# Expert tiles spread over four rounds each, results scattered by token: attention and a mixture of experts on one core

## What is computed

```
# attention, 16 heads of 8
scores = einsum('bhid,bhjd->bhij', q, k) / sqrt(D) * cos_mat
w = softmax(scores); w = (w + roll(w, 1)) / sqrt(2)
out = (w @ v) @ Wo
# experts: 8, the two best for each token, weights = softmax of their two logits
top_logits, idx = top_k(logits, 2); scores = softmax(top_logits)
h1 = x_rep @ w1[e].T; a, g = split(h1, 2)
he = (silu(a) * g) @ w2[e].T          # only where expert_ids == e
combined = (out * scores).sum over the two choices
```

## Time and profile before

| | |
|---|---|
| median of 3 runs | 619.6 us (619.36 to 619.75) |
| time of the profiled execution | 618.71 us |
| its span, first to last instruction | 616.7 us |
| PE busy | 558.7 us (91%) |
| ACT busy | 523.8 us (85%) |
| DVE busy | 200.1 us (32%) |
| POOL busy | 86.5 us (14%) |
| mean granted clock of PE | 0.98 |

### The profile page before, as it was taken

The page is one execution under the profiler, slowest core; times in us unless marked ns, Lnnn a source line. Parts: engine busy times, 40 slices in busy tenths (PEclk is TensorE's granted clock), DMA queues, the critical chain, the costliest instruction groups (busy, mean ns, idle before and its releaser), DMA issues.

```text
span 616.7 us, 19178 instructions
## 1 busy us (share of the span) xinstructions
PE 558.7 (91%) x8012; PEld 260.5 (42%) x8012; DVE 200.1 (32%) x493; ACT 523.8 (85%) x487; POOL 86.5 (14%) x95
## 2 busy tenths in 40 slices
PE   2968988898899999999999999999999988888885
PEld 1433322232355545555555555555455432233334
DVE  7954550200122434334243433424344100000413
ACT  2758879999698988989999898989988899999991
POOL 5200053445100000000000000000000044450000
PEclk9978997899899999999999999999999999999999
DMA  8650052212664333333423234342331011110002
GB/s 231 190 193 10 5 138 78 71 37 70 165 166 131 91 93 87 110 111 91 131 81 104 86 111 112 96 121 75 108 93 49 15 32 31 36 35 10 3 1 72
DMA packets 58666, 53.49 MB, mean 87 GB/s; under 512 B 28188, under 2 KB 48182, under 8 KB 58322
## 3 DMA queue, kind: packets, MB, share of 16 engines
q1 hardware_dynamic: 56082, 47.73, 27.5%
q0 software_dynamic: 2048, 4.20, 2.3%
q10 hardware_dynamic: 448, 0.30, 0.3%
HBM read 38.55 MB, written 13.63 MB: 85 GB/s over the span
## 4 chain that ended last, share of the span: by engine, by line
PE 67%; ACT 15%; issue 11%; DMA 2%; SPq 2%; DVE 2%; ACTq 0%; DVEq 0%
PE ps L1308 32%; PE ps L1282 20%; ACT big L681 14%; PE ps L1219 6%; PE ps L1229 4%; PE ps L1121 2%; PE ps L1315 1%; DMA qk_parts<-store 1%; DVE store L767 1%; DMA acc<-in_L_attn_x 1%; PE ps L1257 1%; ACT second L642 1%; SPq L431 1%; PE ps L1106 1%; DMA store<-in_L_ffn_w 0%
## 5 line engine op out<-in xcount | busy, mean ns | idle before, releaser
L681 ACT ACTIVATE big<-ps 128x1536 f32<-128x1536 f32 (+1 forms) x410 | 480.6, 1240 | 49.6 <-PE ps L1282 47.3
L1308 PE MATMUL ps<-big,vh 128*32 128x256 f32 (+1 forms) x3968 | 270.0, 397 | 0.0
L1282 PE MATMUL ps<-qa,ka 49*128 49x512 f16 x896 | 166.8, 391 | 28.1 <-ACT big L681 19.5
L1308 PEld LDWEIGHTS ps<-big,vh 128*32 128x32 f32 x3968 | 108.2, 110 | 120.3 <-issue 73.8
L1282 PEld LDWEIGHTS ps<-qa,ka 49*128 49x128 f16 x896 | 37.5, 94 | 141.1 <-ACT big L681 98.7
L1219 PE MATMUL ps<-xgT,store 128*32 128x128 f32 x1716 | 65.5, 273 | 2.4 <-DMA store<-in_L_ffn_w 2.4
L1219 PEld LDWEIGHTS ps<-xgT,store 128*32 128x32 f32 x1716 | 53.9, 110 | 17.5 <-issue 5.4
L565 POOL COPY vh<-vaug 128x144 f32 x16 | 6.6, 411 | 338.2 <-PE ps L1308 320.8
L935 DVE SCALAR_TENSOR_TENSOR cs<-cs,ps 128x384 f32<-128x384 f32 x39 | 21.6, 554 | 93.2 <-ACT cs L673 93.2
L971 DVE COPY osb<-ps 128x512 f32<-128x512 f32 x16 | 11.0, 688 | 113.9 <-PE ps L1308 113.8
L988 DVE TENSOR_REDUCE m<-ps 128x1 f32<-128x512 f32 x64 | 44.1, 689 | 5.4 <-PE ps L1325 5.4
(11 more groups left out here) (166 smaller groups left out, 212.0 us busy)
## 6 DMA issues: line engine op xcount, KB each, us to landing
store<-in_L_ffn_w SPq DMA_DIRECT2D x39, 352.0 KB, 3.0
store<-in_L_ffn_w SPq DMA_DIRECT2D x39, 192.0 KB, 3.4
qk_parts<-store SPq DMA_DIRECT2D x8, 512.0 KB
qa<-qk_parts SPq DMA_DIRECT2D x27, 128.0 KB
slots_x<-vh SPq DMA_DIRECT2D x5, 512.0 KB, 6.1
cs<-slots_x SPq DMA_DIRECT2D x80, 32.0 KB, 2.5
slots_y<-y SPq DMA_DIRECT2D x19, 128.0 KB, 3.0
ka<-qk_parts SPq DMA_DIRECT2D x31, 64.0 KB, 2.3
```

The costliest lines, as they stand in the source:

```text
L681: nc.scalar.activation(probs[:, prob_of(tiles[0]):prob_of(tiles[-1]) + 1, :], ps[:, bank_of(tiles[0]):bank_of(tiles[-1]) + 1, :], ACT.Exp, ...
L1282: ins = nc.tensor.matmul(ps[:, bank_of(n), :], k[at:at + KQ, P * o:P * o + P], q[at:at + KQ, CW * c:CW * c + CW], start=True, stop=True, t ...
L1308: ins = nc.tensor.matmul(ps[32 * c:32 * c + 32, O_BANKS[p % 2], cols], vh[:, p % 2, o + 8 * b, :], probs[:, prob_of(n), cols], start=k == ...
```

## The change

- `expert_step` gives a tile four rounds, the steps in the first three and none in the fourth. EXPERTS_AT goes from 41 to 37, so that tiles run in rounds 37 to 193.
- PAIR_EXP_AT goes from 3 to 0, TOP_EXP_AT from 12 to 7, RANK_AT from 8 to 7, SCATTER_AT from 16 to 11.
- Each row of `slots_x` has 132 elements in place of 128: the token's two weights, its first slot and its number (`place_tokens` in round 8, four small copies after `gates`). The zeros that fill `slots_x` go out in 8 DMAs in place of 5, and one more constant is loaded.
- SP loads those four elements of every row (`carried`, 39 pieces of 16 bytes on each of 128 partitions) behind the weights of the first three tiles. From them DVE works out in round 40 each row's weight and the DRAM row for its result (`rows_of_results`, ten instructions on 128x39).
- `result_out` multiplies by that weight. POOL scatters each tile's result to DRAM `results` by token and choice (`scatter_result`, 39 indirect DMAs); `store_results` and the 32 gathers are gone.
- At the end of SP's rounds four plain DMAs of 512 KB load the results, and DVE adds them in 8 instructions (`add_results`, in program order at quad 252, behind `normalise` of head 14).
- `load_exact_shifts` stands at round 156 of SP's program in place of its end.

```diff
-PAIR_EXP_AT = 3
-TOP_EXP_AT = 12
-RANK_AT = 8
+PAIR_EXP_AT = 0
+TOP_EXP_AT = 7
+RANK_AT = 7
+GATES_AT = 8
-EXPERTS_AT = 41
-SCATTER_AT = 16
-ROUNDS_A_PAIR = 6
+EXPERTS_AT = 37
+SCATTER_AT = 11
+ROUNDS_A_TILE = 4
...
-            pair_of, at = divmod(r - EXPERTS_AT, ROUNDS_A_PAIR)
-            m, step = 2 * pair_of + at // 3, at % 3
-            return (m, step) if 0 <= m <= TILES and at < 6 else (None, None)
+            m, step = divmod(r - EXPERTS_AT, ROUNDS_A_TILE)
+            return (m, step) if 0 <= m <= TILES and step < 3 else (None, None)
...
                     for first in range(STAGES - 1):
                         stage_weights(first)
+                    sp.dma_start(carried[:], slots_x[0:TILES * P, DM:WITH_PLACE].rearrange("(n p) k -> p n k", p=P)).then_inc(carried_ld, 16)
...
+            def load_results():
+                for i in range(4):
+                    sp.wait_ge(y_wr[i], -(-(TILES - i) // 4) * 16)
+                for q in range(4):
+                    sp.dma_start(gathered[:, 4 * q:4 * q + 4, :, :], results_v[:, 4 * q:4 * q + 4, :, :]).then_inc(results_ld, 16)
...
+            def scatter_result(m):
+                if m == 0:
+                    pool.wait_ge(rows_of_ready, 1)
+                pool.wait_ge(y_copied, m + 1)
+                nc.gpsimd.indirect_dma_start(results, bass.IndirectOffsetOnAxis(ap=row_of[:, m:m + 1], axis=0),
+                                             y[:, m % 4, :], None).then_inc(y_wr[m % 4], 16)
...
-                nc.vector.tensor_copy(y[:, m % 4, :], ps[:, SIDE_BANK, FP:FP + DM]).then_inc(y_copied, 1)
+                nc.vector.tensor_scalar(y[:, m % 4, :], ps[:, SIDE_BANK, FP:FP + DM], weight_of[:, m:m + 1], None,
+                                        ALU.mult).then_inc(y_copied, 1)
...
-                if r == EXPERTS_AT - 1:
-                    gates()
+                if r == GATES_AT:
+                    place_tokens()
+                if r == EXPERTS_AT + 3:
+                    rows_of_results()
```

More of the change, by code:

```diff
@@ L54 @@
 FP = NF * P
+WITH_PLACE = DM + 4
 ROWS = 2 * D
@@ L88 @@
 EARLY = HALF_HEADS - EXACT
-GATHER_AT = 200
+EXACT_AT = 156
+ADD_AT = 12
 ISQ8 = float(1.0 / np.sqrt(D))
@@ L433, in load_rows, with load_exact_shifts @@
                                  ).then_inc(xg_ld[half], 16)
[L435 to L440, removed]
+            def load_results():
[3 more added lines that the diff above has]
+                    sp.dma_start(gathered[:, 4 * q:4 * q + 4, :, :], results_v[:, 4 * q:4 * q + 4, :, :]).then_inc(results_ld, 16)
+            def load_exact_shifts():
+                sp.wait_ge(exact_shift_ready, 1)
+                for r in range(EXACT):
+                    for half in range(2):
+                        sp.dma_start(qe[64 * half:64 * half + 1, r, :].rearrange("o (t p) -> o t p", p=P),
+                                     exact_shift[NT * r:NT * r + NT, :]).then_inc(exact_shift_ld, 16)
             def stage_weights(m):
@@ L505, in _ @@
                     load_rows(m // 2 + 2)
[L506 to L514, removed]
+                if r == EXACT_AT:
+                    load_exact_shifts()
+            load_results()
             def attend_whole():
@@ L580, in _ @@
             pool.wait_ge(slot_ready, 1)
+            pool.wait_ge(placed, 4)
             def scatter_rows(j):
@@ L583, in scatter_rows @@
                 nc.gpsimd.indirect_dma_start(slots_x, bass.IndirectOffsetOnAxis(ap=slot[:, r, t:t + 1], axis=0),
-                                             xn[:, t, :], None).then_inc(scattered, 16)
+                                             xn_placed[:, t, :], None).then_inc(scattered, 16)
+            result_at = {RING * result_round(m) // NC + 1: m for m in range(TILES)}
             for w in range(SCATTER_AT, H * QUADS):
@@ L596, in _ @@
                     head_values(w // QUADS + 1)
[L597 to L605, removed]
+                if w in result_at:
+                    scatter_result(result_at[w])
         @block.scalar
@@ new lines, in rows_of_results @@
+            def rows_of_results():
+                dve.wait_ge(carried_ld, 16)
+                gate_1, gate_2, first_slot, token = (carried[:, :, k] for k in range(4))
+                here, spare = places[:, NT:NT + TILES], places[:, NT + TILES:NT + 2 * TILES]
+                then(nc.vector.tensor_tensor(choice[:, 0, :], first_slot, here, ALU.is_equal))
+                then(nc.vector.tensor_tensor(choice[:, 1, :], first_slot, here, ALU.not_equal))
+                then(nc.vector.tensor_tensor(choice[:, 2, :], choice[:, 0, :], gate_1, ALU.mult))
+                then(nc.vector.tensor_tensor(choice[:, 3, :], choice[:, 1, :], gate_2, ALU.mult))
+                then(nc.vector.tensor_tensor(weight_of[:], choice[:, 2, :], choice[:, 3, :], ALU.add))
+                then(nc.vector.scalar_tensor_tensor(choice[:, 2, :], token, -2.0, choice[:, 1, :], ALU.add, ALU.add))
+                then(nc.vector.scalar_tensor_tensor(choice[:, 3, :], token, 0.0, choice[:, 2, :], ALU.is_gt, ALU.mult))
+                then(nc.vector.scalar_tensor_tensor(choice[:, 4, :], token, 0.0, spare, ALU.is_equal, ALU.mult))
+                then(nc.vector.tensor_tensor(choice[:, 2, :], choice[:, 3, :], choice[:, 4, :], ALU.add))
+                nc.vector.tensor_copy(row_of[:], choice[:, 2, :]).then_inc(rows_of_ready, 1)
@@ L968, in copy_out, with add_results @@
+            def add_results():
+                dve.wait_ge(results_ld, 4 * 16)
+                for r in range(2):
+                    for q in range(4):
+                        if r == 1:
+                            dve.wait_ge(y_added, q + 1)
+                        here = acc[:, 4 * q:4 * q + 4, :]
+                        nc.vector.tensor_tensor(here, here, gathered[:, 4 * q:4 * q + 4, r, :], ALU.add).then_inc(y_added, 1)
             def copy_out(p):
@@ L1017, in _ @@
                         make_exact_shift(p)
-                    if p == H - 1 and k == JOB_QUAD:
-                        for j in range(2 * NT):
-                            add_result(j)
+                    if p == H - 1 and k == ADD_AT:
+                        add_results()
                 if step == 0:
```

71 lines of the change are left out of this document (38 added, 33 removed).

## The result

| | before | the change |
|---|---|---|
| median of 4 runs each | 619.67 us (619.36 to 620.84) | **610.71 us** (610.23 to 611.72) |
| ratio | | **0.9854**, 95% interval 0.9835 to 0.9873 |
| time of the profiled execution | 618.71 us | 611.17 us |
| its span | 616.69 us | 609.37 us |
| mean granted clock of PE | 0.980 | 0.973 |

Forecast were 609.2, between 604 and 614. The profiled executions are 7.5 us apart and the medians 9.0.

The account below looks back on a forecast made before the run. PE was taken as the bound for the 117 expert rounds and ACT behind them. Terms -12.1 + 2.0 + 0.3 + 0 - 0.6 = -10.4 took 618.71 to 608.3 us, median 609.2, range 604 to 614.

Parts of the forecast that it names:

- Four rounds a tile: Expert rounds: four rounds take 10.30 us in place of 10.61, -0.31 over 39 tiles, -12.1 us; bounds -29 and -3.5.
- heads: Expert rounds: three more head changes, 0.66 us each, fall in PE-bound rounds, +2.0 us, ends 0 and +2.0.
- the wait of 0.22: Expert rounds: PE waits 0.22 us for ACT to free a bank, in a round following one of about 2.4 or less.
- the fourth round gives nothing: Rival on expert rounds: each even round keeps a wait, a tile takes 10.6, heads' 2 us are paid: 620 us, chance 0.06.
- The way to the first tile: First widening, round 38: PE stands 2.7 us until the weights land, +0.3 us against before, ends -4 and +3.
- The carried rows: Load of 4992 pieces behind three tiles' weights: landed at 160 to 162, on the edge, 0 us, ends 0 and +4.
- The price by count: Load of the carried rows: priced by number of pieces, from 5120 pieces taking 7.41 us, at 7.2 us.
- The pair exponential: Early rounds: moving it from round 4's way to behind round 0 saves 0.6 us, ends -1.0 and 0.
- The ranks then come in time for round 7: Early rounds: with the pair exponential moved, the ranks are ready for round 7; no size given.
- Results: End of kernel: the results' load and eight additions finish by 594, before the last head's sum at 602.36, so 0 us.
- slower: PE's clock: Rival: a light round in every four idles PE, half-clock stretches cost 5 us a stage, 624 us with three; chance 0.05.
- The start stands no longer: Rival at the first widening: weights land before 149, the 2.7 us wait and half clock go, -4.5, 605 us; chance 0.12.

Follow-up runs that it names:

- experiment 1: The change with three rounds a tile in place of four, the carried rows' ten instructions one round earlier: 621.73 us, ratio 1.0024 to before.
- experiment 2: The change with EXPERTS_AT 38 in place of 37, so each tile's light round has two pieces of values: 628.74 us, ratio 1.0128 to before.
- Experiment 4: On one chip, the change unedited: 607.97 us; and the change with the first tiles' weights loaded ahead of the first rows: 602.99 us.
- experiment 7: The change with only PAIR_EXP_AT put back from 0 to 3: 611.92 us, ratio 0.9926 to before.
- experiment 6: The change with the front's numbers as before (pair exponential 3, top 12, rank 8, scatter 16, experts 41): 611.18 us, ratio 0.984 to before.
- experiment 5: The change with EXPERTS_AT 39 in place of 37: 605.11 us, ratio 0.9747 to before; with EXPERTS_AT 45: 617.13 us, ratio 0.9959.
- experiments 3: The change with SP staging the first three tiles' weights ahead of the rows: 605.55 us, ratio 0.9769 to before.

## Why the prediction held, and where it was off

Forecast were -10.4 us. The medians moved by 9.0 and the spans of the two profiles by 7.3; only the second can be followed through rows. The fourth round gave about what was forecast. What is missing lies in the clock (points 2 and 6) and in point 4.

1. **Four rounds a tile, -12.1, and heads, +2.0.** The period of 10.30 came out at 10.29, round by round. Round 38 to 204 took 8.86 us less; 1.6 more were lost at the start of the tiles (point 2), so tiles and heads gave 10.4, for 10.1 forecast. The period measured makes -12.5 over 39 tiles, which leaves +2.0 for the heads; no run separates the two. Taking the fourth round back (experiment 1) gives 9.1 and not 10.4, so 1.3 us of this are not shown to be its doing. The reasoning (the wait of 0.22 follows a round of 2.4 or less, and the pieces' parity decides where) also gave the sign of experiment 2 and nearly its size (628.7 for 632). The rival "the fourth round gives nothing, 620" is excluded by experiment 1.

2. **The way to the first tile, +0.3: mis-sized.** The stall itself was right (3.02 for 2.7). Both of its ends came some 2 us later than forecast (PE at 150.8, the weights at 153.8), most of it because round 38 began 1.6 us later than before. The step that failed is "the clock then falls or not as before". It fell for 6.8 us and not 3.4. The two rounds around the stall took 7.51 and 4.39, 6.65 over their steady 5.25; before, 7.23 and 3.31, 5.06 over theirs. So +1.6, of which 0.6 are the longer stall and 1.0 the clock. Experiment 4 shows that this varies by execution: where the half clock lasted 3.4 us, rounds 38 and 39 took 1.4 less.

3. **The carried rows, 0.** Landed before 161.3, as taken (160 to 162), and on the edge, as said: a wait of 0.28 us, none of it on PE. The price by count, 7.2 us, met the 7.5 from issue to landing, but by luck: it is not what the load itself takes. In the trace's DMA records the first piece ran 2.1 us behind the issue, with pieces of the weights ahead of it; the 4992 pieces ran from 155.9 to 159.2, 3.3 us; and DVE started 2.1 us behind the last. The Trainium skill (DMA: Bandwidth & Descriptors, the measured 10.5 ns a packet) gave 3.3 us, with the packets shared out over 16 engines, a step of the prediction's own; the trace agrees. By the same page's 512 bytes as the least for full rate these pieces should be slow, and they were: 80 KB in 3.3 us are 24 GB/s, where the stretch at 92.5 moved 240. With so few bytes that cost nothing.

4. **The pair exponential, -0.6: its size not settled, and its larger part not priced.** Round 0 to 4 gained 0.26 between the two profiles, and 0.75 in experiment 7 against the change beside it. The eight profiles with the exponential in round 0 and a start on time took 12.37 to 12.81 us there, the three with it in round 3 12.76, 12.87 and 13.37, so no pair settles it. The timeline of the change shows why it is not the whole 1.06: the exponential of pairs (43.76, 1.06 us) pushes round 1, and before round 3 ACT still waits for PE, longer than before (2.16 for 2.10):

```profile
41.50 2.37 ACT L694 ACTIVATE big<-ps 128x1536 f32<-128x1536 f32 x2 [1.62 <-PE ps L1320]
...
43.76 1.06 ACT L716 ACTIVATE pair<-pair 128x1024 f32<-128x1024 f32 x1
...
51.86 4.62 ACT L694 ACTIVATE big<-ps 128x1536 f32<-128x1536 f32 x4 [2.16 <-PE ps L1320]
```

   "The ranks then come in time for round 7" had no price. It is worth 3.3 us in rounds 4 to 8, of which 1.4 are given back by round 38, and only because the change asks for the ranks a round earlier (experiment 7 against 6).

5. **Results, 0.** From the last scatter to the first addition 11.4 us, for the 11 taken; eight additions 4.91 for 6; a cover of 11.5 for 8. "If this cover went, each us is on the path" is what experiment 5 shows: 8.4 us open with a start eight rounds later.

6. **Not foreseen: +0.67 ahead of round 0 and +1.22 between rounds 4 and 38.** The first lies in one place of the prologue: four turns of `attnT` took 1.12 us at 15.90, and 0.66 at 15.75 before, the two lengths that such turns have at half and at full clock in experiment 5. (The view's clock reads 1.00 at both, so half clock is argued here and not read.) The change again, in experiment 4, came to round 0 at 42.31, so this part moves by more than 0.67 from one execution to the next. The second is the half-clock stretch at 92, in which 24 matmuls of values took 2.79 for 1.50:

```profile
91.14 0.60 PE L1320 MATMUL ps<-qa,ka 49*128 49x512 f16 x3 [1.32 <-ACT big L694]
...
92.59 2.79 PE L1346 MATMUL ps<-big,vh 128*32 128x256 f32 x24
```

   PE had waited 1.32 us for ACT; before it waited 1.42 in the same place without the clock falling:

```profile
91.07 0.60 PE L1282 MATMUL ps<-qa,ka 49*128 49x512 f16 x3 [1.42 <-ACT big L681]
```

   Other profiles divide the 1.22 us. Rounds 4 to 8 take 9.75 us in all nine profiles with the front of the change, for 9.32 in the two with the front as before: 0.43 are the change's. Rounds 8 to 38 take 84.9 to 85.1 us in the six profiles with the stretch at 92, and 83.6 to 84.1 in the three with the same 10.2 us of half clock in one piece (before, experiment 6, the start in round 45). The change again has no stretch at 92 and takes 83.2. So the other 0.8 us vary by execution. The rival "slower: PE's clock" named this mechanism, but tied it to the light rounds, and there it did not occur: 1.00 for 406 us.

7. **"The start stands no longer", 605**, was the rival nearest to what can be had. It did not happen by itself, since the weights stand behind the rows in SP's order; with that order turned it happened, and gave 5.0 us for the 4.5 worked out. At 0.9769 and 0.9747 of before, experiments 3 and 5 (start in round 39) beat both kernels.

8. **The chances.** The last two are exchanged in the sum of the verdicts: "clock" (0.05, 624) is the slower one, and "nothing gained" (0.06, 620) the one that is the same.

## What to carry to other kernels

Where two engines take turns over a small ring, price a round by its own pattern of work and waits, not by the busy sum: the same 9.86 us of PE's work took 10.29 or 10.94 by which round was left light. Ahead of the first item of a pipeline, look in the loading queue for loads that wait behind others without needing to; moving them cost nothing here and gave back the stall and the slow clock behind it. And treat a constant that feeds a due time together with that due time: alone it looked worth 0.3 us and was worth 4 by the medians.

## What the chip showed that was not expected

- The half-clock stretch behind a wait of some 3 us had different lengths in two executions of one kernel: 6.8 us behind a wait of 3.02, 3.4 behind one of 3.13. Over all profiles it came behind each wait of 2.42 us and more at the first widening, and not behind the one of 1.14.
- A long wait near the end slows the tail as well: with 9.19 us of waiting (experiment 5, round 45) PE ran at half clock for 10.2 us, until 605.9.
- 4992 pieces of 16 bytes ran in 3.3 us, 0.7 ns a piece over all engines, and the load had landed 7.5 us behind its issue.
